# Accumulating expert outputs by indirect DMA tile by tile, with the down projection three units behind the up projection

## The reference

```python
gvals, gidx = jax.lax.top_k(scores, K)          # K = 2, E = 8
gvals = gvals / jnp.clip(gvals.sum(-1, keepdims=True), EPS)
...
    keep = pos < cap                            # cap = 2 * 8192 / 8 = 2048
...
gvals = gvals * keep
disp = jnp.zeros((E, cap, D), x.dtype).at[e_flat, p_flat].add(x_rep * kmask[:, None])
h = jax.nn.gelu(jnp.einsum('ecd,edh->ech', disp, w1) + b1[:, None, :], approximate=False)
y = jnp.einsum('ech,ehd->ecd', h, w2) + b2[:, None, :]
yk = y[e_flat, p_flat]
out = (yk * w[:, None]).reshape(N, K, D).sum(axis=1)
```

## Time and profile before

| | us |
|---|---|
| median of 3 runs | 4508.24 (4508.11 to 4510.07) |
| the profiled execution | 4515.06 |
| its span, on which all times of the trace are counted | 4513.3 |
| PE busy over the span | 3588.2 (80%) |
| DVE busy | 3366.9 (75%) |
| ACT busy | 2318.5 (51%) |
| POOL busy | 1558.9 (35%) |
| first scatter of f2 | 2018.0 |
| first start of a turned output's copy, and the last | 2203.0, 2557.2 |
| first gather, last gather | 2560.6, 2733.6 |

### The profile page before, as it was taken

One profiled execution on the slowest core, in us unless ns is written; L12 is line 12 of the kernel. 1 busy time (PEld: TensorE's weight loads), 2 busy tenths in 40 slices (PEclk: granted clock), 3 DMA queues, 4 the chain that ended last, 5 costly groups with the idle time before them and its releaser, 6 DMA issues. The chain is left out here.

```text
span 4513.3 us, 95409 instructions
## 1 busy us (share of the span) xinstructions
PE 3588.2 (80%) x31831; PEld 2498.6 (55%) x31831; DVE 3366.9 (75%) x6253; ACT 2318.5 (51%) x4148; POOL 1558.9 (35%) x906
## 2 busy tenths in 40 slices
PE   4984979996897999930477505999869999699999
PEld 2553646665564666630355303666546666577777
DVE  5888879997897888860244325888877878688888
ACT  2432657773674666610233203677656666366665
POOL 1210045550002555427200265555244544122222
PEclk9985989996898999955678756999979999699999
DMA  4000022221001222111111112222221211200000
GB/s 131 15 28 23 0 64 64 64 62 54 1 0 42 58 60 56 43 43 52 47 42 47 46 47 59 61 57 61 65 48 45 55 46 44 72 15 14 14 14 14
DMA packets 161161, 200.26 MB, mean 44 GB/s; under 512 B 37948, under 2 KB 109952, under 8 KB 159809
## 3 DMA queue, kind: packets, MB, share of 16 engines
q1 hardware_dynamic: 152769, 180.75, 14.9%
q0 software_dynamic: 8192, 16.79, 1.3%
HBM read 52.96 MB, written 33.55 MB: 19 GB/s over the span
## 5 line engine op out<-in xcount | busy, mean ns | idle before, releaser
L709 ACT ACTIVATE a_p<-a_p 128x480 f32<-128x480 f32 x832 | 501.6, 603 | 517.2 <-DVE a_p L557 514.8
L353 POOL TENSOR_TENSOR a_km<-a_k,a_slots 96x1920 fp32r<-96x1920 f32 x186 | 631.7, 3415 | 179.5 <-DMA a_k<-a_kh 179.5
L552 DVE TENSOR_REDUCE a_mx<-a_sc 128x4 f32<-128x480 f32 (+1 forms) x832 | 542.4, 652 | 128.4 <-PE a_sc L797 98.9
L557 DVE TENSOR_TENSOR a_p<-a_sc,a_mx 128x480 f32<-128x480 f32 x832 | 531.3, 639 | 18.8
L715 ACT ACTIVATE a_pt<-a_tp 120x512 f32<-120x512 f32 x832 | 487.7, 586 | 84.3 <-PE a_tp L806 79.1
L806 PE MATMUL a_tp<-ident,a_p 128*120 128x128 f32 x3328 | 511.0, 276 | 4.1 <-ACT a_p L709 2.3
L806 PEld LDWEIGHTS a_tp<-ident,a_p 128*120 128x120 f32 x3328 | 401.2, 138 | 89.9 <-ACT a_p L709 27.1
L791 PE MATMUL a_sc<-a_km,a_qr 96*128 96x480 f32 x768 | 396.2, 516 | 33.4 <-DMA a_qr<-a_ql 29.3
L830 PE MATMUL a_nd<-a_pt,a_vm 120*32 120x128 f32 x6656 | 354.8, 285 | 0.0
L830 PE MATMUL a_nd<-a_pt,a_dm 120*32 120x128 f32 x6656 | 334.6, 273 | 0.0
L763 PE MATMUL a_pj<-a_ctx,a_wk 128*128 128x480 f32 x128 | 73.1, 655 | 251.8 <-DMA a_ctx<-in_ctxT 251.8
(11 more groups left out here) (426 smaller groups left out, 9124.8 us busy)
## 6 DMA issues: line engine op xcount, KB each, us to landing
a_qr<-a_qh SPq DMA_DIRECT2D x384, 64.0 KB, 2.0
a_k<-a_kh SPq DMA_DIRECT2D x384, 60.0 KB, 2.0
a_ctx<-in_ctxT SPq DMA_DIRECT2D x64, 240.0 KB, 2.7
a_qr<-a_ql SPq DMA_DIRECT2D x192, 64.0 KB, 2.0
a_k<-a_kl SPq DMA_DIRECT2D x192, 60.0 KB, 2.0
dispatched<-zero SPq DMA_DIRECT2D x8, 1024.0 KB, 10.2
f_xr<-dispatched SPq DMA_DIRECT2D x32, 256.0 KB, 2.8
expert_rows<-f_yo SPq DMA_DIRECT2D x32, 256.0 KB, 2.0
```

Source lines behind the costliest of these rows:

```text
L353: v.tensor_tensor(KM[par][:, i, :, :].rearrange("p b (j k) -> p b j k", k=KN), K3[:, i, :, :].unsqueeze(2).to_broadcast([TR, GB, 4, KN]), ...
L552: v.tensor_reduce(mx[:], view, AX.X, ALU.max).then_inc(mx_ready, 1)
L557: v.tensor_tensor(PR[s % 4][:].rearrange("p (h k) -> p h k", k=k), view, mx[:].unsqueeze(2).to_broadcast([P, heads, k]), ALU.subtract).the ...
L709: a.activation(PR[s % 4][:], PR[s % 4][:], ACT.Exp).then_inc(exp_ready, 1)
```

## The change

The outputs are no longer stored and gathered. `dispatched` gets two more words per row (ROW = 130): the weight of the row's token, and the token's number. x is first stored to a DRAM table `summed`. After each tile POOL issues four indirect DMAs that add the 512 output rows, scaled by their weights on ACT, to the rows of `summed` that the token numbers name; at an expert's first tile it first waits for all earlier adds. At the end SP loads x back from `summed` in eight parts, and DVE computes the statistics. Rows without a token have weight 0 and a number beyond the tokens; for this the table is written from a buffer `empty` instead of zeros, now in the first expert phase f0. The weight has one word in a row, so the second half of the scatters waits until the first half has landed and the word is rewritten. f_xr has four buffers; the load of tile t waits for the adds of tile t - 4, since these read the token numbers in its buffer. LAG is 3 (with four buffers for f_ah and f_al). The turning of a tile's outputs, `sums_turn(t)`, stands in unit 0 of tile t + 2 instead of unit 3 of tile t + 1, and `outs(t)` in unit 1 of tile t + 2.

```diff
@@ load_phase
-                sp.wait_ge(zeros, 1)
-                view = R.dispatched[0:E2 * CAP, :].rearrange("(i p r) d -> i p r d", p=P, r=16)
-                for i in range(E2 * CAP // (16 * P)):
-                    sp.dma_start(view[i], R.zero[:].unsqueeze(1).to_broadcast([P, 16, D])).then_inc(R.dispatch_zeroed, 16)
@@ gated_rows_phase (f0)
+            if kind == "proto":
+                @block.sync
+                def _(sp):
+                    sp.wait_ge(empty_ready, 2)
+                    table = R.dispatched[0:E2 * CAP, :].rearrange("(i p r) w -> i p r w", p=P, r=16)
+                    for i in range(E2 * CAP // (16 * P)):
+                        sp.dma_start(table[i], empty[:]).then_inc(table_empty, 16)
+                    sp.wait_ge(table_empty, 16 * (E2 * CAP // (16 * P)))
...
+                if kind == "proto":
+                    nc.gpsimd.memset(empty[:], 0.0).then_inc(empty_ready, 1)
+                    pool.wait_ge(empty_ready, 1)
+                    nc.gpsimd.iota(empty[:].bitcast(I32)[:, :, D + 1], [[1, 16]], base=NB * P,
+                                   channel_multiplier=16).then_inc(empty_ready, 1)
@@ dispatched_experts_phase
-    LAG = 2
+    LAG = 3
...
+        def adds(t):
+            return 64 * (t // 4 + 1)
@@ POOL
-                pool.wait_ge(placed, 2)
-                pool.wait_ge(R.dispatch_zeroed, 16 * (E * CAP // (16 * P)))
+                nc.gpsimd.iota(X.rows[:].bitcast(I32)[:, :, D + 1], [[P, NB]], base=0,
+                               channel_multiplier=1).then_inc(ids_ready, 1)
+                pool.wait_ge(ids_ready, 1)
+                pool.wait_ge(placed, 1)
                 for i in range(2):
+                    pool.wait_ge(weighted, i + 1)
                     for b in range(NB):
                         nc.gpsimd.indirect_dma_start(
...
-                for i in range(2):
-                    pool.wait_ge(stored[i], 8 * NT)
-                for b in range(NB):
-                    at_least(pool, Z["x_added"], b - AHEAD + 1)
-                    for i in range(2):
+                pool.wait_ge(x_kept, 16 * PARTS)
+                for t in range(NT):
+                    pool.wait_ge(Z["yo_ready"], t + 1)
+                    if t % (NT // E) == 0:
+                        for before in range(max(0, t - 4), t):
+                            pool.wait_ge(R.added[before % 4], adds(before))
+                    for j in range(4):
                         nc.gpsimd.indirect_dma_start(
-                            out=YG[:, 2 * (b % AHEAD) + i, :], out_offset=None, in_=R.expert_rows[:, :],
-                            in_offset=bass.IndirectOffsetOnAxis(ap=source[:, i, b:b + 1], axis=0)).then_inc(gathered[b % AHEAD], 16)
+                            out=R.summed[:, :],
+                            out_offset=bass.IndirectOffsetOnAxis(ap=XR[t % 4][:].bitcast(I32)[:, j, D + 1:D + 2], axis=0),
+                            in_=YO[t % 2][:, j, :], in_offset=None, compute_op=ALU.add).then_inc(R.added[t % 4], 16)
@@ SP
+                def load(t):
+                    if t >= 4:
+                        sp.wait_ge(R.added[t % 4], adds(t - 4))
+                    sp.dma_start(XR[t % 4][:], tile_of(R.dispatched, t)).then_inc(xr_in[t % 4], 16)
+
+                for i in range(PARTS):
+                    sp.dma_start(view[:, part(i), :], R.x[:, part(i), :]).then_inc(x_kept, 16)
+                sp.wait_ge(R.scattered, 16 * 2 * NB)
                 for t in range(NT):
-                    if t + 2 < NT:
-                        load(t + 2)
-                    sp.wait_ge(Z["yo_ready"], t + 1)
-                    sp.dma_start(tile_of(R.expert_rows, t), YO[t % 2][:]).then_inc(stored[t % 2], 16)
+                    load(t)
+                for t in range(NT - 4, NT):
+                    sp.wait_ge(R.added[t % 4], adds(t))
+                for i in range(PARTS):
+                    sp.dma_start(R.x[:, part(i), :], view[:, part(i), :]).then_inc(x_in[i], 16)
@@ DVE
+                v.tensor_copy(X.rows[:, :, D], X.weight[:, 0, :]).then_inc(weighted, 1)
+                dve.wait_ge(R.scattered, 16 * NB)
+                v.tensor_copy(X.rows[:, :, D], X.weight[:, 1, :]).then_inc(weighted, 1)
...
                 for b in range(NB):
...
+                    if b % (NB // PARTS) == 0:
+                        dve.wait_ge(x_in[b // (NB // PARTS)], 16)
+                    v.bn_stats(R.stats[:, b, :], R.x[:, b, :]).then_inc(R.stats_done, 1)
@@ ACT
                 def outs(t):
                     act.wait_ge(Z["po_ready"], t + 1)
-                    at_least(act, stored[t % 2], (t // 2) * 16)
-                    a.activation(YO[t % 2][:], PO[t % 2][:], ACT.Copy).then_inc(Z["yo_ready"], 1)
+                    if t >= 2:
+                        act.wait_ge(R.added[(t - 2) % 4], adds(t - 2))
+                    for j in range(4):
+                        last = a.activation(YO[t % 2][:, j, :], PO[t % 2][:, j, :], ACT.Identity,
+                                            scale=XR[t % 4][:, j, D:D + 1])
+                    last.then_inc(Z["yo_ready"], 1)
...
-                    if c == 3 and t > 0:
-                        outs(t - 1)
+                    if c == 1 and t > 1:
+                        outs(t - 2)
@@ PE
-                    if c == 3 and t > 0:
-                        sums_turn(t - 1)
+                    if c == 0 and t > 1:
+                        sums_turn(t - 2)
```

More of the change, by code:

```diff
@@ L39 @@
 CAP = 2 * NB * P // E2
-AHEAD = 8
+ROW = D + 2
+SPARE = 16 * P
 def at_least(eng, sem, value):
@@ L901, in __init__ @@
         if by_rows:
-            self.rows = sb(name + "_rows", [P, NB, D])
+            self.rows = sb(name + "_rows", [P, NB, ROW])
             self.slots = sb(name + "_slots", [P, 2, NB])
@@ L1039, in turn @@
                     for j in range(GB):
-                        h = X.rows[:, g * GB + j, :] if X.by_rows else H[par][:, j, :]
+                        h = X.rows[:, g * GB + j, 0:D] if X.by_rows else H[par][:, j, :]
                         last = t.transpose(TR[par][:, j * P:(j + 1) * P], h, R.ident[:])
@@ L1141, in ln_group @@
                     if X.by_rows:
-                        norm.apply(dve, g, X.rows[:, bass.ds(g * GB, GB), :]).then_inc(h_ready, 1)
+                        norm.apply(dve, g, X.rows[:, bass.ds(g * GB, GB), 0:D]).then_inc(h_ready, 1)
                         return
@@ L1309, in gated_rows_phase @@
         GBL = BL - UNG
+        if kind == "proto":
+            empty = sb(n_("empty"), [P, 16, ROW])
+            empty_ready, table_empty = sem(n_("empty_ready")), sem(n_("table_empty"))
         def lagged(g, c, par, first, lag, f):
@@ L1884, in dispatched_experts_phase @@
         place = sb(n_("place"), [P, 2, NB], I32)
-        source = sb(n_("source"), [P, 2, NB], I32)
-        XR = [sb(n_(f"xr{i}"), [P, 4, D]) for i in range(2)]
+        XR = [sb(n_(f"xr{i}"), [P, 4, ROW]) for i in range(4)]
         XH = [sb(n_(f"xh{i}"), [P, TR], F32R) for i in range(2)]
@@ L1889, in dispatched_experts_phase @@
         A = [sb(n_(f"a{i}"), [P, TR]) for i in range(2)]
-        AH = [sb(n_(f"ah{i}"), [P, TR], F32R) for i in range(3)]
-        AL = [sb(n_(f"al{i}"), [P, TR], F32R) for i in range(3)]
+        AH = [sb(n_(f"ah{i}"), [P, TR], F32R) for i in range(4)]
+        AL = [sb(n_(f"al{i}"), [P, TR], F32R) for i in range(4)]
         YS = sb(n_("ys"), [P, TR])
         YO = [sb(n_(f"yo{i}"), [P, 4, D]) for i in range(2)]
-        YG = X.rows
         PU = [ps(n_(f"pu{i}"), [P, TR]) for i in range(2)]
@@ L1899, in dispatched_experts_phase @@
         spare_ready, index, placed = sem(n_("spare_ready")), sem(n_("index")), sem(n_("placed"))
[L1900 to L1901 removed]
+        ids_ready, weighted, x_kept = sem(n_("ids_ready")), sem(n_("weighted")), sem(n_("x_kept"))
+        xr_in, x_in = [sem(n_(f"xr_in{i}")) for i in range(4)], [sem(n_(f"x_in{i}")) for i in range(PARTS)]
         Z = {s: sem(n_(s)) for s in ("px_ready", "xh_ready", "xl_ready", "up_ready", "a_ready", "hi_ready", "lo_ready",
[L1903 removed]
+                                     "dn_ready", "ys_ready", "po_ready", "yo_ready")}
         tile_of = lambda rows, t: rows[t * TR:(t + 1) * TR, :].rearrange("(p r) d -> p r d", r=4)
+        def adds(t):
+            return 64 * (t // 4 + 1)
         def unit(n):
@@ L1932, in load @@
+                part = lambda i: slice(i * NB // PARTS, (i + 1) * NB // PARTS)
                 def load(t):
[L1933 to L1938, removed]
-                for t in range(NT):
-                    if t + 2 < NT:
-                        load(t + 2)
-                    sp.wait_ge(Z["yo_ready"], t + 1)
-                    sp.dma_start(tile_of(R.expert_rows, t), YO[t % 2][:]).then_inc(stored[t % 2], 16)
+                    if t >= 4:
+                        sp.wait_ge(R.added[t % 4], adds(t - 4))
+                    sp.dma_start(XR[t % 4][:], tile_of(R.dispatched, t)).then_inc(xr_in[t % 4], 16)
@@ L2090, in build @@
```

(8 more changed lines are left out.)

34 lines of the change are left out of this document (12 added, 22 removed).

## The result

The change made the kernel slower by a third of a per cent: 4525.22 us (median of 7 runs, 4520.65 to 4529.98) against 4510.07 (7 runs, 4506.01 to 4516.20) of the kernel before; ratio 1.0033, 95% interval [1.0021, 1.0045]. The forecast was 4486, faster, with 4450 to 4560 as its range: the time lies in the range, on the other side of no change.

What follows compares the result with a forecast made beforehand. It took TensorE as busiest in the tile loop, with POOL issuing indirect DMAs one by one in the stages around it. −25.3 + 1 + 1.9 = −22.4 us took the median from 4508.24 to 4486; range 4450 to 4560.

Steps and rivals of the forecast that it cites:

- Start: Program start: zeroing leaves the load phase, so the next phase issues at 19.15 instead of 39.46 and gains 5 more; −25.3 us.
- the sum with f0: Program start plus first expert phase: −25.3 us from moving the zeroing, +1 for writing the table of empty rows; −24.3.
- Scatter: Scatters before the tile loop: POOL's wait between the halves +1.4 us, second numbering +0.3; together +1.7.
- The closed chain, once per tile: Tile loop: each tile's adds wait behind a load that waits for the previous tile's adds, however many buffers turn; 17.6 us.
- Rival 3: Tile loop doesn't stall: buffers free in time, TensorE bounds a tile at about 7.5 us; 4203; chance 0.03.
- The period, 17.6: Tile loop, f_px to next f_px: 16.4 us with adds at a scatter's cost, +0.8 destination read, +0.4 on POOL.
- I add 0.1 per add on POOL: Tile loop, POOL's four adds per tile: each holds POOL 0.1 us longer than a scatter, 0.4 on the period.
- rival 4: Tile loop: adds are free beyond a scatter, period 16.4 us, −58, 4450; chance within the 0.50 for periods below 18.05.
- What stands around the loop: Before and after the closed turns: f_px of tile 4 at 2220.7 before the start's gain; 12 trailing adds 18.6 us, x's reading 16.2.
- the forecast −22.4: Whole kernel: −25.3 at the start, +1 for the table, +1.9 for the expert stage; −22.4 us.
- Rival 1: Tile loop: an add holds POOL 0.48 us longer, period 19.1, total +22, 4530; decides from 18.7; chance 0.34.
- The Trainium skill's rule on casts: Tile loop: POOL cannot write DMA descriptors during VectorE's float32 SBUF copies; up to 1.7 us per period, about 50 in all.

## Why the prediction was wrong, point by point

- *Start*: −25.3 forecast, 23.7 less at the last constant, 24.1 less at the first scatter where −24.3 was the sum with f0. Right; alone it is worth 19 us in the medians.
- *Scatter*, +1.7: first f_px at 2164.0 instead of 2186.36, 22.4 earlier, so 24.1 − 22.4 = 1.7. Right.
- *The closed chain, once per tile*: right in every link, and shown by opening it (4252) and by closing it over two tiles (4308). Rival 3 was rightly set aside for this kernel.
- *The period, 17.6*: this is the step that failed, and in it the price of the addition, the term "I add 0.1 per add on POOL". Measured are 1.86 us from add to add where a scatter has 1.26, so 0.6. Three steps are 5.59 us (2410.62 to 2416.21) where I had 3.87 + 0.4; landing is 3.3 where I had 2.2 + 0.8. That is +1.6 a turn. The plain writes measure the term by itself: with them the kernel takes 4443, where the sum at a scatter's price (rival 4) had 4450, and the additions cost 82 us where I had 29.6 × 1.2 = 36. So all else in the sum was right to 7 us, and the 46 us too little for the addition turned the sign. Two links were shorter than I had them: f_po 0.71 instead of 1.1, load to f_px 2.73 instead of 2.9. The turn shown has 18.7, the mean is 18.4, and 27 × (18.4 − 17.6) = 22 us.
- *What stands around the loop*: f_px of tile 4 at 2202.12 where the sum had 2220.7 − 24.3 = 2196.4, +5.7, since the copies ended 3.5 us later than I had them and the first adds, which start beside a cast and f_al, took up to 2.1 us; and 57.5 us from f_px of tile 31 to the phase a3 (2699.01 to 2756.56) where I had 51, +6.4: mostly the 12 trailing adds at 0.5 us more each.
- Together 22 + 5.7 + 6.4 = 34 above the forecast −22.4: +11.5 at the start of a3 (2756.56 − 2745.10), and the medians say +15.
- *Rival 1* happened: a holding time half as long again. I had put 0.48 on each add as its upper bound, and it is 0.6; the landing was dearer too. By its price (+22) the forecast would have been 4530. The 18.7 from which the rival decides was reached in single turns, not in the mean (18.4); the kernel is slower all the same, because the surroundings of the loop cost 12 us more as well. The Trainium skill's point that the reduction of a collective emits two read descriptors where a copy emits one (Collectives: The Full Stack, "The bandwidth ceiling") spoke for it. The traces agree only so far as that an add has more packets: q0, POOL's queue, has 22528 with adds and 8192 with plain writes, which is 144 for each add and 32 for each write or scatter. That is 4.5 times as many, which a second read does not explain. I should have leaned on the bound, and it was itself too low: the add was the one operation that the trace did not show, in the one place where 1 us costs 30. That the time lies in the stated range is owed to this rival, for which the range was drawn that wide, and not to the forecast.
- *The Trainium skill's rule on casts* (SBUF — State Buffer, "SBUF: two separate sides") would have put up to 1.7 us on a period. The traces agree with the rule for adds that start beside a cast: 49 of them take 1.68 us in the mean, in four kernels, and f_al holds adds up in the same way. But it is worth little in the stalled loop, since nearly all adds start when VectorE runs neither (11 of 128 do not), and a cast that begins after the add's start does not matter there (2410.62 takes 1.56 with one inside it): all 128 adds together are 2.1 us above 1.56 each, 0.07 a tile instead of 1.7. With the chain open it is 13 us of the kernel with eight buffers.
- What the change gains and loses, by the experiments: the table gains 19 us; gathers and additions gone and the adds in their place, with the loop stalled for want of buffers, lose 34 (15 + 19). With the chain open the adds, with the third unit of lag, gain some 100 us, which is an estimate: the kernel before with four buffers has 4368, less 19 for the table 4349 (no run has both), against 4245.

## What to carry to other kernels

When a buffer's release is moved behind a longer path (here from the turning of its rows to the landing of an add that reads its indices), write down the closed chain: who waits for the release, what that waiter stands ahead of on its engine, and whether the release of the next buffer lies behind it. Its length divided by the number of tiles that it spans is the least that a tile can take, whatever the engines could do; here one more tile of span took 217 us off the kernel, where the dearest part of the chain, the additions, gave 82. An operation that the trace does not show, on such a chain, should be measured first: even the upper bound that I set for the add was too low, and its price, four times in each of 28 rounds, turned a gain (4443 with plain writes) into a loss (4525).

## What the runs showed of the hardware

- An indirect DMA of 128 rows of 512 bytes that adds to DRAM holds POOL 1.56 us and lands 3.3 us after its start (stalled loop); the plain write of the same rows holds it 0.96 and lands in 2.2. Each add has 144 packets on the queue, each write 32.
- Adds grow with a dense loop: 1.57 us in the mean in the stalled loop (201.3 us for 128), 1.66 with eight buffers. What makes them longer is VectorE: an add that starts while VectorE runs a float32 cast or a two-input instruction from SBUF to SBUF ends 1.43 us after that instruction, up to 2.1 us after its own start; beside f_xl, which reads f_px, or beside nothing it takes 1.56.
- The granted clock of the tile stage was 0.71 with waits of 8.4 us per tile, 0.80 with waits of 3 us, 0.95 without. In the turn shown it was 0.50 (1.2 GHz) from 2403.60 to 2408.70, behind f_px's wait, with products 0.43 us from start to start, and 1.00 (2.4 GHz) from 2409.20 to 2412.00, with 0.23.
